# Cross-attention with its row sums computed among the values, reciprocals turned by transfers, and outputs normalized and projected four heads at a time

## The chip, the core and the metric

The kernel runs on one core of a Trainium2 chip. A core has five engines that run side by side: TensorE for matmuls (PE in the profile; its weight loads are PEld), VectorE (DVE), ScalarE (ACT), GpSimd (POOL) and SyncE (SP), which here only issues transfers. They meet at semaphores. Matmuls write to PSUM, eight banks of 128 partitions by 512 floats; all else lives in SBUF. The metric is the device time of one execution in microseconds (us), lower being better.

## What is computed

The reference is two layers on 1024 tokens of width 128, each an attention over a context of 6404 rows (width 96) and a mixture of experts. The change lies in the second attention and what follows it at once:

```python
q = (x @ Wq).reshape(B, S, HEADS, DIM_HEAD).transpose(0, 2, 1, 3)      # 8 heads of 64
k = (context @ Wk).reshape(B, L, HEADS, DIM_HEAD).transpose(0, 2, 1, 3)
v = (context @ Wv).reshape(B, L, HEADS, DIM_HEAD).transpose(0, 2, 1, 3)
attn = jnp.einsum('bhsd,bhld->bhsl', q, k) * scale
attn = jax.nn.softmax(attn, axis=-1)
out = jnp.einsum('bhsl,bhld->bhsd', attn, v)
out = out.transpose(0, 2, 1, 3).reshape(B, S, INNER)
return out @ Wo + bo
```

The result is added to x; a layer norm and the last mixture of experts follow.

## The kernel before, in words

**Stages.** A start (loads, layer norm, first projections), the maxima of the first attention's scores and the value projection for all heads (values go to a DRAM scratch), the first attention, the first experts, a stretch in which the maxima of head 0 are found, then the second attention from 347 to 1326 us of the span, then the second experts. Each engine has its own program, written out by hand in the order in which it runs; there is no scheduler. An instruction that waits holds up all that is behind it on its engine.

**The second attention.** The 6404 context rows are 51 tiles of 126. The loop runs over 8 heads (h) and, in each, over 13 blocks (b) of four tiles (the last has three). In a block PE does, in this order: the scores of tiles against all 1024 queries, two halves of 512 (`scores1`, L1406 and L1407, the second matmul adding the low parts and the shift by the row's maximum); two steps of the maxima of the next head (`max_scores`, L1372); the product with the values for each tile (`attend1`, L1419, one matmul for each half of the queries, into the two halves of the partitions of bank 7); after the first tile of these the key projection for a later head (`k_proj_parts`, L1359); and two more maxima steps. ACT takes exp of each score bank (`exps`, L718) and rounds the projected keys (L683). DVE reduces the maxima steps from PSUM (`maxima`, L959), makes the low parts of the keys (L949) and adds the exps of one tile in four to the second half of the row sums (`add_rows`, L1011, L1016); POOL adds the rest (L527, L531) and folds DVE's part in (L536). From here on, "head 2, block 4" is h = 2, b = 4; a block is counted from its first L1406 to that of the next. A block with nothing special in it is called plain.

**What is done once a head**, in the middle of blocks after the third tile's scores: in block 1 the row sums of the head before (`sum_rows`, eight matmuls that have 128 columns of the summed exps as weights and one column of ones as data, L1432) and their reciprocals on DVE (L980); in blocks 2 and 3 the output projection of the head before (`project_out`, L1444, two halves of four matmuls each) and on DVE the scaled addition to x (`add_output`, L990); in blocks 5 and 6 a query projection for two heads on (L1351, L671, L943); in block 12 the shifts of the next head: DVE's row maxima are turned by one matmul (`row_shift`, L1377, into bank 5), and DVE spreads them over eight rows of q_low (`shift`, L970). Bank 5 is also one of the two banks of the maxima step behind, so that step waits for DVE. ACT copies the head's output from bank 7 to `acc_raw` (L692). `c_reduced`, `c_exped`, `c_shift`, `c_x`, `c_out` are the semaphores by which PE waits for maxima, exps, shifts and additions.

**SP** issues all transfers in one order: at each head's start the values of a later head (1.6 MB), then wq and wk.

**Where PE waits for DVE in each block.** The bank of the fourth score (tile 1, second half) and of the fifth are those of the first maxima step, and after the third tile's scores PE waits for both steps; so a DVE that is late with the maxima holds PE up.

## Time and profile before

| | us |
|---|---|
| three runs | 1439.64, 1443.58, 1443.79 |
| median | 1443.58 |
| the profiled execution, its own time | 1445.09 |
| its span, first to last instruction | 1443.3 |
| TensorE, mean granted clock | 0.975 |

The span is 1.8 us shorter than that execution's own time. Busy shares say that PE is nearly always occupied, but a busy PE is not one at its peak, as its matmuls overlap. What a once-a-head piece costs is read best from the length of its block against a plain one.

### The profile page before, as it was taken

What the parts mean: (1) busy time and instruction counts of PE and PEld (TensorE: products, weight loads), DVE (VectorE), ACT (ScalarE), POOL (GpSimd) and SP (SyncE); (2) the same over time, 40 slices, a digit from 0 to 9 for tenths busy, and PEclk for the clock granted to TensorE, in tenths of its full rate; (3) what the DMA queues carried; (4) which work ended last, traced back from release to release, by engine and by line L of the source; (5) the groups of instructions that cost most, each with busy time, mean ns of one, the idle gap of its engine ahead of it and who ended that gap; (6) DMA issues with size and microseconds to landing.
All of it is one profiled execution on the core that took longest, in us unless ns stands there. A gap on an engine that the chain in (4) does not pass through costs nothing.

```text
span 1443.3 us, 20175 instructions
## 1 busy us (share of the span) xinstructions
PE 1382.9 (96%) x6309; PEld 797.2 (55%) x6309; DVE 1095.1 (76%) x1484; ACT 796.0 (55%) x1580; POOL 943.4 (65%) x543
## 2 busy tenths in 40 slices
PE   5989998887999999999999999999999999999898
PEld 3867776533455555555555555555555555555665
DVE  8976666597887778788777978787887887676655
ACT  3458887322565555556555555555555565554432
POOL 5001112342889889888988988898888899887110
PEclk8999999966999999999999999999999999999999
DMA  6640000400000200200020020002002000000011
GB/s 172 206 134 17 17 17 8 92 4 0 1 1 1 50 1 1 49 1 1 1 50 1 1 49 1 1 1 50 0 1 47 0 1 0 1 1 13 19 41 39
DMA packets 77373, 39.46 MB, mean 27 GB/s; under 512 B 62047, under 2 KB 70000, under 8 KB 77002
## 3 DMA queue, kind: packets, MB, share of 16 engines
q1 hardware_dynamic: 77290, 38.36, 10.6%
q8 instruction: 52, 0.85, 0.2%
q14 instruction: 31, 0.25, 0.1%
HBM read 24.66 MB, written 13.68 MB: 27 GB/s over the span
## 4 chain that ended last, share of the span: by engine, by line
PE 87%; DVE 7%; DMA 3%; ACT 2%; issue 1%; POOL 0%; SPq 0%; ACTq 0%; DVEq 0%; POOLq 0%
PE ps L1419 25%; PE ps L1406 15%; PE ps L1407 13%; PE ps L1372 9%; DVE chunk_max L959 3%; DMA v_scratch<-v_stage 3%; PE ps L1359 3%; PE ps L1577 2%; PE ps L1239 2%; PE ps L1240 2%; PE ps L1241 2%; PE ps L1228 2%; PE ps L1230 2%; PE ps L1229 2%; PE ps L1563 1%
## 5 line engine op out<-in xcount | busy, mean ns | idle before, releaser
L531 POOL TENSOR_TENSOR psums<-psums,probs 126x1024 f32<-126x1024 f32 (+1 forms) x392 | 821.6, 2096 | 122.9 <-ACT probs L718 75.4
L718 ACT ACTIVATE probs<-ps 126x512 f32<-126x512 f32 (+1 forms) x816 | 416.9, 617 | 290.5 <-PE ps L1407 287.0
L959 DVE TENSOR_REDUCE chunk_max<-ps 128x2 f32<-128x1008 f32 (+1 forms) x416 | 472.5, 1181 | 75.7 <-PE ps L1372 74.3
L1419 PE MATMUL ps<-probs,v_mem 126*64 126x512 f32 (+1 forms) x1632 | 389.6, 598 | 0.0
L1406 PE MATMUL ps<-q_heads,ring 128*126 128x512 f32 (+1 forms) x816 | 343.1, 420 | 1.2
L1407 PE MATMUL ps<-q_low,ring 128*126 128x512 f32 (+1 forms) x816 | 322.6, 395 | 0.0
L1011 DVE TENSOR_TENSOR xn<-xn,probs 126x512 f32<-126x512 f32 x126 | 231.8, 1840 | 29.9 <-ACT probs L718 25.6
L683 ACT CAST ring<-ps 64x252 fp32r<-64x252 f32 (+1 forms) x356 | 128.4, 361 | 136.2 <-PE ps L1359 133.0
L1419 PEld LDWEIGHTS ps<-probs,v_mem 126*64 126x64 f32 (+1 forms) x1632 | 111.5, 136 | 165.5 <-issue 121.2
L1406 PEld LDWEIGHTS ps<-q_heads,ring 128*126 128x126 f32 (+1 forms) x816 | 152.1, 186 | 88.4 <-issue 43.9
L1372 PE MATMUL ps<-ring,q_heads 64*128 64x504 f32 (+1 forms) x416 | 169.3, 475 | 19.1 <-DVE chunk_max L959 10.6
L1407 PEld LDWEIGHTS ps<-q_low,ring 128*126 128x126 f32 (+1 forms) x816 | 153.0, 188 | 32.8 <-issue 2.9
L1372 PE MATMUL ps<-ring,q_low 64*128 64x504 f32 (+1 forms) x416 | 169.3, 475 | 0.0
L1372 PEld LDWEIGHTS ps<-ring,q_heads 64*128 64x128 f32 x416 | 70.1, 194 | 160.1 <-issue 71.6
L485 POOL TENSOR_TENSOR wv_lo<-vslot,wv_hi 126x97 fp32r<-126x97 f32 x51 | 20.4, 399 | 185.9 <-DVE wv_hi L858 185.9
L863 DVE TENSOR_TENSOR q_shift<-probs,q_all 126x512 fp32r<-126x512 f32 x102 | 70.5, 693 | 58.8 <-ACT q_all L612 58.6
L949 DVE TENSOR_TENSOR ring<-ps,ring 64x252 fp32r<-64x252 f32 (+1 forms) x178 | 73.7, 414 | 34.4 <-ACT ring L683 32.2
L1372 PEld LDWEIGHTS ps<-ring,q_low 64*128 64x128 f32 x416 | 70.1, 194 | 0.0
L612 ACT ACTIVATE q_all<-ps 126x512 fp32r<-126x512 f32 x102 | 60.9, 599 | 11.1 <-PE ps L1241 1.4
L605 ACT ACTIVATE probs<-ps 126x512 f32<-126x512 f32 x102 | 60.7, 601 | 9.7 <-PE ps L1230 2.9
L829 DVE TENSOR_REDUCE chunk_max<-ps 128x1 f32<-128x378 f32 x136 | 63.1, 542 | 2.1 <-PE ps L1194 2.0
L540 POOL TENSOR_TENSOR parts<-pair_w,parts 128x256 fp32r<-128x256 f32 x17 | 11.9, 703 | 73.8 <-ACT parts L744 73.8
(212 smaller groups left out, 1422.7 us busy)
## 6 DMA issues: line engine op xcount, KB each, us to landing
v_scratch<-v_stage SPq DMA_DIRECT2D x51, 252.0 KB
v_mem<-v_scratch SPq DMA_DIRECT2D x8, 1606.5 KB
ctx_mem<-in_ctx_t SPq DMA_DIRECT2D x3, 803.2 KB, 8.8
vslot<-in_ctx_rows SPq DMA_DIRECT2D x51, 47.2 KB
pair_w<-in_f_pairs SPq DMA_DIRECT2D x17, 128.0 KB, 2.1
pair_w<-in_f_pairs SPq DMA_DIRECT2D x17, 65.0 KB, 1.8
x_tok<-in_x SPq DMA_DIRECT2D x1, 512.0 KB, 4.2
wo<-in_c_wo SPq DMA_DIRECT2D x1, 512.0 KB
```

The source lines that it names most:

```text
L531: pool.tensor_tensor(sums[0:r, 0:width], sums[0:r, 0:width], probs[0:r, n % PROBS, 0:width], ALU.add).then_inc(c_sum, 1)
L683: ins = act.copy(ring[half * HD:(half + 1) * HD, g % RING, tiles, 0, :], ps[part * HD:(part + 1) * HD, bank, 0:(tiles.stop - tiles.start) ...
L718: act.activation(probs[0:r, n % PROBS, cols(half)], ps[0:r, score_bank(t, half), :], ACT.Exp, scale=float(HD) ** -0.5).then_inc(c_exped, 1)
L829: dve.tensor_reduce(chunk_max0[:, i, g:g + 1], ps[:, i % 4, 0:CK], AX, ALU.max).then_inc(max_reduced, 1)
L863: dve.tensor_tensor(p_lo[:, cols(half)], probs0[:, j, cols(half)], f32(p_hi[:, cols(half)]), ALU.subtract).then_inc((a_plo0, a_padd)[half] ...
L949: ins = dve.tensor_tensor(ring[HD:P, g % RING, tiles, 1, :], ps[rows, bank, 0:(tiles.stop - tiles.start) * KT] .rearrange("p (n k) -> p n ...
L959: dve.tensor_reduce(chunk_max[:, h % 2, i:i + 2, c], ps[:, banks[0]:banks[1] + 1, 0:group_tiles(c) * KT], AX, ALU.max).then_inc(c_reduced, 1)
L1011: dve.tensor_tensor(sums[0:r, :], sums[0:r, :], new[0:r, :], ALU.add).then_inc(c_sumd, 1)
L1372: pe.matmul(ps[:, banks[half], 0:group_tiles(c) * KT], q[rows, h % 3, tile_cols(i + half)], ring[rows, g % RING, 0:group_tiles(c), 0, :], ...
L1406: pe.matmul(s, ring[:, g % RING, j, 0, 0:r], q_heads[:, h % 3, cols(half)], start=True, stop=False)
L1407: pe.matmul(s, ring[:, g % RING, j, 1, 0:r], q_low[:, h % 3, cols(half)], start=False, stop=True).then_inc(c_scored, 1)
L1419: ins = pe.matmul(ps[half * HD:(half + 1) * HD, B_ACC, :], v_tiles[0:r, h % 2, t, :], probs[0:r, n % PROBS, cols(half)], start=(t == 0), s ...
```

## The change

1. `sum_rows` becomes, for heads 0 to 6, two matmuls with ones (126 by 64) as weights and 512 columns of summed exps as data, so that each of 64 partitions holds all sums of a half; they stand behind the key projection among the value products of block 1 and write to bank 1 (for head 6 bank 5). ACT copies the bank to SBUF (`sums_out`).
2. SP turns the sums by way of DRAM (`turn_sums`): a write of 2 rows of 512, a read back as 128 by 8 (32 bytes a partition), DVE's reciprocal of 128 by 8 in block 2 behind the row additions, a write of these, and two reads that spread them over 64 partitions each.
3. DVE multiplies the head's output (128 by 512, in SBUF) by them in block 4 (`normalize`). The outputs of four heads stay in `acc`.
4. The output projections of heads 0 to 3 are done at once, in head 4, block 7, added up in PSUM over the heads; DVE adds two banks to x. Those of heads 4 to 7 follow the last block, head 7 on its own and scaled as before.
5. `row_shift` goes to bank 1, one of the banks of the scores, ahead of the third tile's scores; the maxima step behind no longer waits for the shift.
6. The first loads of the experts' weights (pair_w, four transfers) move from the start to the end of the second attention, and some small buffers change place; the memset of q_low and the flipped identity report by another semaphore.

TensorE, block 12 of a head (L1377 and in the changed program L1434 is the turning of the row maxima, L1406/L1466 the scores of the third tile, L1372/L1429 the maxima steps), before and then changed:

```order
L1406 MATMUL ps<-q_heads,ring 104x512
L1407 MATMUL ps<-q_low,ring 104x512
L1377 MATMUL ps<-neg_ident,row_max 8x128
L1372 MATMUL ps<-ring,q_heads 128x504
L1372 MATMUL ps<-ring,q_low 128x504
L1372 MATMUL ps<-ring,q_heads 128x504
L1372 MATMUL ps<-ring,q_low 128x504
L1419 MATMUL ps<-probs,v_mem 64x512 x2
```
```order
L1434 MATMUL ps<-neg_ident,row_max 8x128
L1466 MATMUL ps<-q_heads,ring 104x512
L1467 MATMUL ps<-q_low,ring 104x512
L1466 MATMUL ps<-q_heads,ring 104x512
L1467 MATMUL ps<-q_low,ring 104x512
L1429 MATMUL ps<-ring,q_heads 128x504
L1429 MATMUL ps<-ring,q_low 128x504
L1429 MATMUL ps<-ring,q_heads 128x504
```
The turning has moved ahead of the third tile's four score matmuls.

TensorE, block 1 of a head (L1432: row sums before; L1489: row sums changed; L1419/L1479: value products; L1359/L1416: key projection), before and then changed:

```order
L1432 MATMUL ps<-ones,psums 128x1 x8
L1406 MATMUL ps<-q_heads,ring 126x512
L1407 MATMUL ps<-q_low,ring 126x512
L1406 MATMUL ps<-q_heads,ring 126x512
L1407 MATMUL ps<-q_low,ring 126x512
L1372 MATMUL ps<-ring,q_heads 128x504
L1372 MATMUL ps<-ring,q_low 128x504
L1372 MATMUL ps<-ring,q_heads 128x504
L1372 MATMUL ps<-ring,q_low 128x504
L1419 MATMUL ps<-probs,v_mem 64x512 x2
L1359 MATMUL ps<-ctx_mem,wk 64x252 x2
```
```order
L1466 MATMUL ps<-q_heads,ring 126x512
L1467 MATMUL ps<-q_low,ring 126x512
L1429 MATMUL ps<-ring,q_heads 128x504
L1429 MATMUL ps<-ring,q_low 128x504
L1429 MATMUL ps<-ring,q_heads 128x504
L1429 MATMUL ps<-ring,q_low 128x504
L1479 MATMUL ps<-probs,v_mem 64x512 x2
L1416 MATMUL ps<-ctx_mem,wk 64x252 x2
L1489 MATMUL ps<-psums,ones 64x512 x2
L1479 MATMUL ps<-probs,v_mem 64x512 x6
```
The row sums have left the scores and stand among the value products, as two matmuls in the place of eight.

VectorE, blocks 2 to 4 (L990: scaled addition to x; L1011/L1065: row additions; L1018: reciprocals; L1026: normalize; L959/L999: maxima; L949/L989: low parts of keys), before and then changed:

```order
L959 TENSOR_REDUCE chunk_max<-ps 128x2 x2
L990 SCALAR_TENSOR_TENSOR x_tok<-ps,rden,x_tok 128x128 x4
L1011 TENSOR_TENSOR xn<-xn,probs 126x512
L959 TENSOR_REDUCE chunk_max<-ps 128x2 x2
L949 TENSOR_TENSOR ring<-ps,ring 64x2x126 x2
L959 TENSOR_REDUCE chunk_max<-ps 128x2 x2
L990 SCALAR_TENSOR_TENSOR x_tok<-ps,rden,x_tok 128x128 x4
L1011 TENSOR_TENSOR xn<-xn,probs 126x512
L959 TENSOR_REDUCE chunk_max<-ps 128x2 x2
L949 TENSOR_TENSOR ring<-ps,ring 64x2x126 x2
L959 TENSOR_REDUCE chunk_max<-ps 128x2 x2
L1011 TENSOR_TENSOR xn<-xn,probs 126x512
```
```order
L1065 TENSOR_TENSOR xn<-xn,probs 126x512
L1018 RECIPROCAL rden<-sum_cols 128x8
L999 TENSOR_REDUCE chunk_max<-ps 128x2 x2
L989 TENSOR_TENSOR ring<-ps,ring 64x2x126 x2
L999 TENSOR_REDUCE chunk_max<-ps 128x2 x2
L1065 TENSOR_TENSOR xn<-xn,probs 126x512
L999 TENSOR_REDUCE chunk_max<-ps 128x2 x2
L989 TENSOR_TENSOR ring<-ps,ring 64x2x126 x2
L999 TENSOR_REDUCE chunk_max<-ps 128x2 x2
L1065 TENSOR_TENSOR xn<-xn,probs 126x512
L1026 TENSOR_TENSOR acc<-acc,xn 128x512
L999 TENSOR_REDUCE chunk_max<-ps 128x2 x2
```
The two scaled additions of blocks 2 and 3 are gone; in their place come a reciprocal behind block 2's row addition and a multiplication behind block 4's.

The diff, cut to its core:

```diff
+B_SHIFT = 1
+B_SUMS = (1, 1, 1, 1, 1, 1, 5, 0)
+BATCH, BATCH_AT = 4, 7
...
@@ sync @@
-            for s in range(2):
-                sp.dma_start(pair_w[:, s, 0:2 * P], f1_pairs[s][:, 0:2 * P]).then_inc(g_w13[s], 16)
-                sp.dma_start(pair_w[:, s, 2 * P:PAIR_W], f1_pairs[s][:, 2 * P:PAIR_W]).then_inc(g_w[s], 16)
...
+            def turn_sums(h):
+                sp.wait_ge(c_spread, h + 1)
+                sp.dma_start(sums_dram[h % 2], spread_sums[0:P:HD, h % 2, :]).then_inc(c_turn, 16)
+                sp.wait_ge(c_turn, 80 * h + 16)
+                sp.dma_start(sum_cols[:, :], sums_dram[h % 2].rearrange("a (p j) -> (a p) j", j=TT)).then_inc(c_turn, 16)
+                sp.wait_ge(c_rden, 2 * h + 1)
+                sp.dma_start(rden_dram[h % 2].rearrange("a (p j) -> (a p) j", j=TT), rden[:, :]).then_inc(c_turn, 16)
+                sp.wait_ge(c_turn, 80 * h + 48)
+                for half in range(2):
+                    sp.dma_start(spread_sums[half * HD:(half + 1) * HD, h % 2, :],
+                                 rden_dram[h % 2, half:half + 1, :].to_broadcast([HD, HALF])).then_inc(c_turn, 16)
+            next_weights(2)
+            for h in range(2, HEADS + 1):
+                if h < HEADS:
+                    sp.wait_ge(c_attended, TILES * (h - 1))
+                    sp.dma_start(v_tiles[:, h % 2], v_dram_v[h]).then_inc(c_vload[h % 2], 16)
+                if h + 1 < HEADS:
+                    next_weights(h + 1)
+                turn_sums(h - 2)
@@ scalar @@
-                if h:
-                    act.wait_ge(c_out, 2 * h)
-                act.copy(acc_raw[:, :], ps[:, B_ACC, :]).then_inc(c_acc, 1)
+                if h >= BATCH:
+                    act.wait_ge(c_out, 1)
+                act.copy(acc[:, h % BATCH, :], ps[:, B_ACC, :]).then_inc(c_acc, 1)
+            def sums_out(h):
+                act.wait_ge(c_sums, h + 1)
+                act.copy(spread_sums[:, h % 2, :], ps[:, B_SUMS[h], :]).then_inc(c_spread, 1)
...
+                    if b == 1 and h:
+                        sums_out(h - 1)
@@ vector @@
             def reciprocals(h):
...
+                if h < HEADS - 1:
+                    dve.wait_ge(c_turn, 80 * h + 32)
+                    dve.reciprocal(rden[:, :], sum_cols[:, :]).then_inc(c_rden, 1)
...
+            def normalize(h):
+                dve.wait_ge(c_turn, 80 * h + 80)
+                dve.wait_ge(c_acc, h + 1)
+                dve.tensor_tensor(acc[:, h % BATCH, :], acc[:, h % BATCH, :], spread_sums[:, h % 2, :],
+                                  ALU.mult).then_inc(c_rden, 1)
+            def add_outputs(n):
+                dve.wait_ge(c_out, 2 * n + 1)
...
+                for half in range(2):
+                    tiles = slice(half * (TT // 2), (half + 1) * (TT // 2))
+                    ins = dve.tensor_tensor(x_tok[:, tiles, :],
+                                            ps[:, PAIRS[1][half], :].rearrange("p (t d) -> p t d", d=D),
+                                            x_tok[:, tiles, :], ALU.add)
...
-                    if b == 1 and h:
-                        reciprocals(h - 1)
-                    if b in (2, 3) and h:
-                        add_output(h - 1, b - 2, PAIRS[1])
+                    if (h, b) == (BATCH, BATCH_AT):
+                        add_outputs(0)
...
+                    if b == 2 and h:
+                        reciprocals(h - 1)
+                    if b == 4 and h:
+                        normalize(h - 1)
...
             reciprocals(HEADS - 1)
-            for part in range(2):
-                add_output(HEADS - 1, part, PAIRS[part])
+            add_last_output()
+            dve.wait_ge(c_x, 2)
+            add_outputs(1)
@@ tensor @@
+                if h and t == 2 * GT and k == B_SUMS[h - 1]:
+                    pe.wait_ge(c_spread, h)
...
+                if h < HEADS - 1:
+                    for half in range(2):
+                        ins = pe.matmul(ps[half * HD:(half + 1) * HD, B_SUMS[h], :], ones[0:KT, 0:HD], psums[:, h % 2, cols(half)],
+                                        start=True, stop=True)
...
+            def project_out(h, banks, first, last):
+                for u in range(TT // 2):
+                    for half in range(2):
+                        rows = slice(half * HD, (half + 1) * HD)
+                        ins = pe.matmul(ps[:, banks[half], tile_cols(u)], acc[rows, h % BATCH, tile_cols(u)], wo1[rows, h, :],
+                                        start=(first and u == 0), stop=last, skip_group_check=True)
+                return ins
...
+                        if b == GROUPS_H - 1 and t % GT == 1 and h + 1 < HEADS:
+                            pe.wait_ge(c_exped, 2 * (TILES * h + b * GT) + B_SHIFT + 1)
+                            row_shift(h + 1, B_SHIFT)
...
-                            if b == 1 and h:
-                                sum_rows(h - 1)
-                            if b in (2, 3) and h:
-                                if b == 3:
-                                    pe.wait_ge(c_x, 2 * h - 1)
-                                project_out(h - 1, b - 2, PAIRS[1])
+                            if (h, b) == (BATCH, BATCH_AT):
+                                pe.wait_ge(c_rden, 2 * BATCH)
+                                for done in range(BATCH):
+                                    ins = project_out(done, PAIRS[1], done == 0, done == BATCH - 1)
+                                ins.then_inc(c_out, 1)
...
-                            if b == GROUPS_H - 1 and h + 1 < HEADS:
-                                row_shift(h + 1)
...
-                        elif b == GROUPS_H - 1 and h + 1 < HEADS:
-                            pe.wait_ge(c_shift, 2 * h + 4)
...
-                        if t % GT == 0 and g is not None:
+                        if t % GT == 0 and (g is not None or (b == 1 and h)):
                             pe.wait_ge(c_exped, 2 * (TILES * h + block_tiles(b)[-1] + 1))
-                            k_proj_parts(g, B_KEYS)
-            pe.wait_ge(c_x, 2 * HEADS - 2)
-            for part in range(2):
-                project_out(HEADS - 1, part, PAIRS[part])
+                            if g is not None:
+                                k_proj_parts(g, B_KEYS)
+                            if b == 1 and h:
+                                sum_rows(h - 1)
+            project_out(BATCH, PAIRS[1], True, False)
+            pe.wait_ge(c_acc, HEADS)
+            project_out(HEADS - 1, PAIRS[0], True, True).then_inc(c_out, 1)
             sum_rows(HEADS - 1)
+            project_out(BATCH + 1, PAIRS[1], False, False)
+            project_out(BATCH + 2, PAIRS[1], False, True).then_inc(c_out, 1)
```

## Rows read from the trace of the kernel before

**Rows 1.** The page's first part: busy us, share, instructions.
```profile
PE 1382.9 (96%) x6309; PEld 797.2 (55%) x6309; DVE 1095.1 (76%) x1484; ACT 796.0 (55%) x1580; POOL 943.4 (65%) x543
```
**Rows 2.** The page's fourth part, the chain that ended last, by engine.
```profile
PE 87%; DVE 7%; DMA 3%; ACT 2%; issue 1%; POOL 0%; SPq 0%; ACTq 0%; DVEq 0%; POOLq 0%
```
**Rows 3.** Stretches: start:end length, busy by engine, clock, DMA; head 2.
```profile
610.98:622.01 11.03, 11.03 (x63) 6.62 (x61) 7.81 (x9) 5.59 (x12) 8.41 (x4) 1.00 0.01 1
622.01:632.18 10.17, 10.17 (x55) 5.42 (x53) 8.61 (x11) 5.59 (x12) 7.73 (x4) 1.00 0.00 1
632.18:642.65 10.47, 10.33 (x54) 5.26 (x53) 9.04 (x12) 5.70 (x12) 8.96 (x5) 1.00 0.01 2
642.65:651.94 9.29, 9.29 (x46) 4.76 (x45) 8.07 (x9) 5.49 (x12) 7.62 (x4) 1.00 0.00 0
...
601.65:728.05 126.40, 125.28 (x605) 66.06 (x603) 100.41 (x105) 73.35 (x159) 109.93 (x52) 1.00 0.07 15
```
**Rows 4.** The same view: head 7, its blocks 1, 2 and 4.
```profile
1234.90:1244.16 9.26, 9.26 (x50) 5.75 (x49) 7.55 (x6) 4.13 (x8) 8.54 (x6) 1.00 0.00 0
1244.16:1252.51 8.35, 8.35 (x42) 4.42 (x41) 5.36 (x8) 4.13 (x8) 7.33 (x6) 1.00 0.01 3
...
1260.84:1268.32 7.48, 7.48 (x34) 3.96 (x32) 5.02 (x4) 4.03 (x8) 5.57 (x5) 1.00 0.00 0
```
**Rows 5.** TensorE in time order, head 2: start, us, line, [idle before <- releaser].
```profile
607.64 2.74 PE L1419 MATMUL ps<-probs,v_mem 126*64 126x512 f32 x12
...
613.86 1.84 PE L1432 MATMUL ps<-ones,psums 126*128 126x1 f32 x16
...
624.99 0.71 PE L1444 MATMUL ps<-wo,acc_raw 64*128 64x128 f32 x8
```
**Rows 6.** TensorE in time order, block 12 of head 2.
```profile
722.04 0.39 PE L1377 MATMUL ps<-neg_ident,row_max 128*8 128x128 f32 x2
722.50 0.50 PE L1372 MATMUL ps<-ring,q_heads 64*128 64x504 f32 x1
...
723.79 0.50 PE L1372 MATMUL ps<-ring,q_heads 64*128 64x504 f32 x1 [0.79 <-DVE q_low L970]
```
**Rows 7.** VectorE in time order, head 2: blocks 4 and 5, then 12.
```profile
645.13 2.49 DVE L1011 TENSOR_TENSOR xn<-xn,probs 126x512 f32<-126x512 f32 x1
...
650.35 0.85 DVE L949 TENSOR_TENSOR ring<-ps,ring 64x252 fp32r<-64x252 f32 x2 [0.49 <-ACT ring L683]
651.85 2.32 DVE L959 TENSOR_REDUCE chunk_max<-ps 128x2 f32<-128x1008 f32 x2 [0.65 <-PE ps L1372]
656.50 0.69 DVE L943 TENSOR_TENSOR q_heads<-ps,q_heads 64x512 fp32r<-64x512 f32 x1 [2.33 <-ACT q_heads L671]
...
722.46 1.28 DVE L970 TENSOR_TENSOR q_low<-ps,diag 8x512 fp32r<-8x512 f32 x2 [1.19 <-PE ps L1377]
```
**Rows 8.** Durations by line, in ns: least, median, most.
```profile
L1011 DVE TENSOR_TENSOR xn<-xn,probs x126: 668/1738/2748, 374.1 to 1325.2; 126x512 f32<-126x512 f32 x125, 104x512 f32<-104x512 f32 x1
...
L531 POOL TENSOR_TENSOR psums<-psums,probs x392: 1271/2367/2725, 354.1 to 1326.3; 126x1024 f32<-126x1024 f32 x132, 126x512 f32<-126x512 f32 x60, 104x1024 f32<-104x1024 f32 x4
...
L929 DVE TENSOR_TENSOR x_tok<-ps,x_tok x2: 681/686/692, 270.7 to 271.3; 128x512 f32<-128x512 f32 x2
```
**Rows 9.** ScalarE in time order, the key casts of head 2, block 4.
```profile
648.82 1.50 ACT L683 CAST ring<-ps 64x252 fp32r<-64x252 f32 x4 [1.29 <-PE ps L1359]
```
**Rows 10.** The transfers: size and median us from issue to landing.
```profile
wq<-in_c_wq SPq DMA_DIRECT2D x8, 64.0 KB, 9.8
out_t<-ctx_mem SPq DMA_DIRECT2D x2, 256.0 KB, 2.0
...
gw<-in_f_gw SPq DMA_DIRECT2D x1, 16.0 KB, 1.6
```
**Rows 11.** All engines in time order, behind the second attention.
```profile
1327.27 1.16 PE L1444 MATMUL ps<-wo,acc_raw 64*128 64x128 f32 x16 [0.78 <-ACT acc_raw L692]
...
1330.66 2.16 DVE L990 SCALAR_TENSOR_TENSOR x_tok<-ps,rden,x_tok 128x128 f32<-128x128 f32 x8
```

114 lines of the change are left out of this document (53 added, 61 removed).

## Prediction, on record before the result was known

> **What bounds the kernel now.** I read the page's busy shares first: PE is busy for 96% of the span, DVE for 76%, POOL for 65% [rows 1]. A busy PE is no proof that it is the bound, so next the chain that ended last: 87% of it is PE [rows 2]. What counts is then how long each block takes, so I cut head 2 into stretches that begin at a block's first score matmul. A plain block (block 4) takes 9.29 us; in it PE is busy throughout, DVE for 8.07 [rows 3]. Block 1, with the row sums of the head before, takes 11.03; blocks 2 and 3, with the two halves of the output projection, 10.17 and 10.47. So these pieces lie in the open, and each costs what its block is longer: 1.74, 0.88 and 1.18 us. The other heads from 1 to 6 show the same blocks. In head 7, where there are no maxima left to find, block 4 takes 7.48, block 1 9.26 and block 2 8.35 [rows 4]: 1.78 and 0.87 more. Block 12 has a hole of its own: after the turning of the row maxima the second maxima step starts 1.29 us behind the first, 0.79 of it idle time that DVE's shift ends [rows 6].
>
> The sum is made against the profiled execution's 1445.1 us, which is 1.5 above the median of the runs, 1443.6; 1.8 of it lie outside the span.
>
> **Row sums.** Sixteen PE instructions (eight matmuls of two passes) in 1.84 us [rows 5] become four of the same shape as the value products of one tile, of which three tiles (twelve instructions) take 2.74 [rows 5]: 0.9 us. Gain in heads 1 to 6: 6 x (1.74 - 0.9) = 5.0; in head 7: 0.9. ACT's copy of the bank goes where ACT has just cast the keys and waits for the next block's scores; ACT is busy for 5.49 of a plain block's 9.29 [rows 3], so it costs nothing.
>
> **Output projection in blocks 2 and 3.** Both go: 6 x (0.88 + 1.18) = 12.4, and in head 7 twice 0.87, 1.7. Their work comes back in two places. The batch in head 4, block 7 has 32 matmuls, 64 instructions; at the rate of the tail (16 in 1.16 us [rows 11]) that is 4.6, at that of a block (8 in 0.71 [rows 5]) 5.7; I take 5.1. Behind it DVE adds two banks, each an addition of 128x512 from PSUM at 0.69 [rows 8], and PE has a tile's scores and one maxima step to do meanwhile, about the same length: 0.4 more. Together 5.5, once.
>
> **Reciprocals by way of DRAM.** DVE now waits in block 2 for a write and a read of 4 KB, and the maxima behind it wait with it. In a plain block DVE is through with the row addition at 645.13 + 2.49 = 647.62, 4.97 us into it [rows 7]. Block 1 will be 10.2 long, so DVE comes to the reciprocals 15.2 us after block 1 began. ACT ends its key casts at 648.82 + 1.50, 7.67 us into a block [rows 9], and copying a bank costs under 0.78 (PE's idle time ahead of the projection of the tail is such a copy [rows 11]): the sums are in SBUF at 8.4. That leaves 6.8 us for two transfers. A write to DRAM of 256 KB lands after 2.0 us, a small read after 1.6 [rows 10], so about 4 with the issues. The wait should be nothing. From both sides: zero, and if each took as long as wq's 9.8 [rows 10], about 12 us a head. I take zero, since wq's is long only because it is issued right behind the 1.6 MB of values; those go at the start of block 0, some 17 us ahead of the sums. The spreading back has two blocks of time. The Trainium skill (DMA: Bandwidth & Descriptors, Anatomy of one DMA) gives some 2.0 us as the fixed cost of a transfer and calls DRAM the slowest target; by it the round trip would be near 4, and with the landings above the trace agrees. The same page's Specifications want pieces of 512 bytes or more and speak of read-modify-write below; the writing back of the reciprocals is in pieces of 32 bytes, and no row here shows what such a write costs.
>
> **Normalizing in block 4.** DVE gains a multiplication of 128x512 with both inputs in SBUF. Its nearest rows are the row additions of 126x512: at least 0.67 us, 1.74 in the middle, 2.75 at most [rows 8]. The spread comes from POOL, which adds 126x1024 at 2.37 at a time nearly without a pause: where a DVE addition falls on a POOL one, it ends after it. The new one directly follows a row addition, so it meets the next POOL addition: 2.4 us is my value; the bounds are 0.67 and 2.37 + 0.67 = 3.04. In a plain block DVE idles for 0.49 and 0.65 [rows 7], 1.14 together. So DVE is 2.4 - 1.14 = 1.3 us late with the maxima of block 5, of which PE, which has a little time there, loses 1.1. A hint that the lateness counts: block 3 has the same PE work as block 2, DVE is busy for 0.43 us more, and the block is 0.30 longer [rows 3]. In block 5 DVE idles 2.33 ahead of the query's low part [rows 7] and catches up. Cost: 6 x 1.1 = 6.6, between 0 and 6 x (3.04 - 1.14) = 6 x 1.9 = 11.4. In head 7 DVE is busy for 5.02 of 7.48 [rows 4], which hides it.
>
> **Shifts by way of a bank of scores.** Head 2's 0.79 us goes [rows 6]: the turning starts some 1 us earlier, DVE, idle 1.19 ahead of the shift [rows 7], starts it as much earlier, and the maxima step no longer shares its bank. The exp of the first tile, for which PE now waits, should be just through. What is late next is DVE's row addition, which then meets POOL at another point; nothing to 0.79 is left. I take all of it, in six heads (0 to 5): 4.7.
>
> **The tail.** The projection of head 4 goes ahead of the wait for ACT's copy: 1.16 for the 0.78 idle [rows 11], 0.4 more. Those of heads 5 and 6 lie beside DVE's reciprocals and additions (2.16 [rows 11]), but then two additions of 0.69 [rows 8] follow in the open: 1.4. Together 1.8. The weights loaded late are used well behind the layer norm. Fewer loads at the start may give up to 1 us; I take none.
>
> **Sum.** Gains 5.0 + 0.9 + 12.4 + 1.7 + 4.7 = 24.7. Costs 5.5 + 6.6 + 1.8 = 13.9. Net 10.8: 1445.1 to 1434.3, and 1443.6 to 1432.8 in terms of the median.
>
> **Rivals.**
> The round trip through DRAM is too long (the slower one). DVE stands in block 2 of heads 1 to 7 with all maxima behind it. It starts to cost when both transfers take more than 6.8 + 1.1 = 7.9 us, and eats up the whole gain at 10.8 / 7 = 1.5 more, 9.4 us, 4.7 for each. At 5 each it would be 7 x 2.1 = 14.7, so 1432.8 + 14.7 = 1447.5. For it: wq's 9.8 us, and no 32-byte write in the trace. Against it: every small transfer with nothing ahead lands in about 2. Chance 0.07.
>
> VectorE becomes the bound. The normalizing costs its upper end, 11.4 for 6.6, and the row addition of block 12, which now starts 1 us earlier, falls on a POOL addition and gives the 4.7 back: 1432.8 + 4.8 + 4.7 = 1442.3. For it: in a head of 126.40 us DVE is busy 100.41 and POOL 109.93 [rows 3], and the head shrinks while both have as much to do. Against it: 11 us of slack are left on POOL even in a head of 121. Chance 0.08.
>
> The normalizing always waits for a whole POOL addition, 2.37 + 0.67 = 3.04, and block 12 keeps its gain: 6 x (1.9 - 1.1) = 4.8 more, 1437.6. For it: the addition before it holds POOL back, so POOL is next when it ends. Against it: 2.75 is the most that any row addition took [rows 8]. Chance 0.12. The Trainium skill (SBUF — State Buffer, Who interferes with whom) has this as a rule: a two-input VectorE operation from SBUF and a GpSimd operation that reads SBUF exclude each other for a whole instruction. The spread of the row additions agrees with it; how the two take turns when DVE has two in a row beside 1024-wide ones, no row shows.
>
> The normalizing falls into a gap of POOL or into DVE's idle time: 0.67 is under 1.14, it costs nothing, 1432.8 - 6.6 = 1426.2. For it: the least of 0.67 does occur. Against it: the row addition before it ends just when POOL goes on. Chance 0.14.
>
> **How the numbers follow.** The forecast has 0.55; the rest, 0.04, is for what I don't see. A change is told from none at about 0.3%, 4.3 us. Faster: forecast, gap and the whole wait (0.81) and half of the unseen, 0.83. Same: the bound case and the other half, 0.10. Slower: 0.07. The range from 1426 to 1440 takes in the gap case and the whole wait and stops short of the bound case.
>
> **What would show it.** Block 1 of head 2 near 10.2 us, blocks 2 and 3 near 9.3, block 5 longer by about 1.1 than now, block 12 shorter by 0.8; the batch block 5.5 us longer; DVE with no wait for a transfer ahead of the reciprocals; the normalizing at 2.4 us. It is wrong if DVE waits for the read of the sums, if a block other than 5 grows, or if the tail costs more than 3 us.

## The result, and the profile after

| | before | changed |
|---|---|---|
| median, us (lowest to highest, 4 runs each) | 1443.37 (1439.64 to 1443.79) | 1429.40 (1427.00 to 1431.47) |
| ratio | | 0.9905, 95% interval 0.9891 to 0.9919 |
| the profiled execution, its own time | 1445.09 | 1430.34 |
| its span | 1443.3 | 1428.5 |
| mean granted clock | 0.975 | 0.975 |

The changed kernel is faster: by 14.0 us in the medians (11.7 to 15.7 by the interval) and by 14.8 between the two traces. Forecast were 10.8, just below that interval, and 1432.8 us; the time lies inside the range of 1426 to 1440. The median before is that of four runs, one more than the prediction had.

First the busy shares of the changed kernel, beside [rows 1].

```profile
PE 1371.8 (96%) x6225; PEld 784.4 (55%) x6225; DVE 1103.8 (77%) x1439; ACT 798.7 (56%) x1587; POOL 944.2 (66%) x543
```

PE is busy for 11.1 us less. DVE is busy for 8.7 more with 45 instructions fewer: 56 scaled additions of 128x128 went, 7 multiplications and 4 additions of 128x512 came. That is the first hint at where part of the gain stays. Next the stretches of the changed kernel, cut at the same instructions as [rows 3] and [rows 4]: head 1 blocks 1 to 5 and the whole head; head 2 block 4 and the whole head; head 4 block 7; head 7 blocks 1 and 2.

```profile
480.38:490.53 10.15, 10.15 (x51) 5.14 (x49) 7.84 (x8) 6.07 (x13) 7.74 (x5) 1.00 0.01 1
490.53:499.78 9.25, 9.25 (x46) 4.83 (x44) 8.17 (x9) 5.48 (x12) 7.66 (x4) 1.00 0.02 3
499.78:509.01 9.23, 9.23 (x46) 4.85 (x44) 8.09 (x8) 5.49 (x12) 8.66 (x5) 1.00 0.12 28
509.01:519.47 10.46, 9.59 (x46) 4.91 (x44) 10.38 (x8) 5.49 (x12) 9.74 (x6) 1.00 0.00 0
519.47:530.26 10.79, 10.61 (x48) 5.21 (x46) 8.43 (x10) 6.19 (x13) 9.27 (x5) 1.00 0.01 2
471.05:595.23 124.18, 122.78 (x576) 63.60 (x574) 102.44 (x98) 73.73 (x160) 110.17 (x52) 1.00 0.08 17
...
633.15:642.38 9.23, 9.23 (x47) 4.84 (x45) 8.90 (x9) 5.49 (x12) 8.66 (x5) 1.00 0.01 2
595.23:717.82 122.59, 122.17 (x577) 63.61 (x575) 95.60 (x98) 73.64 (x160) 110.60 (x52) 1.00 0.08 18
...
911.52:925.06 13.54, 13.54 (x110) 8.40 (x108) 8.62 (x11) 6.59 (x13) 9.30 (x5) 1.00 0.01 1
...
1220.14:1228.65 8.51, 8.51 (x39) 4.16 (x37) 6.85 (x5) 4.61 (x9) 7.79 (x7) 1.00 0.00 0
1228.65:1236.14 7.49, 7.49 (x34) 3.96 (x33) 5.62 (x6) 4.03 (x8) 6.92 (x5) 1.00 0.02 1
```

Blocks 1, 2 and 3 have come down to 10.15, 9.25 and 9.23, the last two to the length of a plain block. Block 4, plain before at 9.29 [rows 3], is now 10.46, with PE busy for only 9.59 of it and DVE for 10.38. Head 2 is the exception: its block 4 is 9.23 and the head 1.6 us shorter than head 1. The block with the batch is 13.54, where heads 1, 3 and 5 have 9.47 or 9.48. The lengths of all heads, cut in this way:

| us | head 0 | 1 | 2 | 3 | 4 | 5 | 6 | 7 (blocks 0 to 11) |
|---|---|---|---|---|---|---|---|---|
| before | 128.10 | 126.51 | 126.40 | 126.40 | 126.74 | 126.41 | 119.82 | 93.31 |
| changed | 126.74 | 124.18 | 122.59 | 124.09 | 128.18 | 124.20 | 118.37 | 90.86 |
| normalizing on GpSimd (below) | 126.87 | 122.63 | 123.25 | 122.62 | 126.71 | 122.63 | 116.80 | 90.86 |

Why block 4 grew is seen in VectorE's time order in the changed kernel, block 4 of head 1 and then of head 2:

```profile
511.28 2.71 DVE L1065 TENSOR_TENSOR xn<-xn,probs 126x512 f32<-126x512 f32 x1
513.91 2.84 DVE L1026 TENSOR_TENSOR acc<-acc,xn 128x512 f32<-128x512 f32 x1
516.68 2.31 DVE L999 TENSOR_REDUCE chunk_max<-ps 128x2 f32<-128x1008 f32 x2
...
635.40 0.72 DVE L1065 TENSOR_TENSOR xn<-xn,probs 126x512 f32<-126x512 f32 x1
636.04 2.87 DVE L1026 TENSOR_TENSOR acc<-acc,xn 128x512 f32<-128x512 f32 x1
```

and in TensorE's, at the end of block 4 of head 1:

```profile
517.93 0.50 PE L1429 MATMUL ps<-ring,q_heads 64*128 64x504 f32 x1 [0.26 <-DVE chunk_max L999]
...
519.04 0.50 PE L1429 MATMUL ps<-ring,q_heads 64*128 64x504 f32 x1 [0.61 <-DVE chunk_max L999]
```

GpSimd's additions beside them, two in head 1 and one in head 2:

```profile
511.03 2.41 POOL L565 TENSOR_TENSOR psums<-psums,probs 126x1024 f32<-126x1024 f32 x1
513.59 2.62 POOL L565 TENSOR_TENSOR psums<-psums,probs 126x1024 f32<-126x1024 f32 x1
...
634.28 1.29 POOL L565 TENSOR_TENSOR psums<-psums,probs 126x512 f32<-126x512 f32 x1
```

In head 1 the row addition and the normalizing (L1026) take 2.71 and 2.84 us in a row, and the maxima start so late that PE waits for them twice, 0.87 together. Each of the two starts while a GpSimd addition is running and ends about 0.55 behind it: 513.99 behind 513.44, 516.75 behind 516.21. In head 2 the row addition, in the same code, starts when GpSimd's addition has 0.17 left and takes 0.72, again ending 0.55 behind it. DVE is 2 us earlier with everything behind it, and PE waits for nothing, though the normalizing itself takes 2.87. What shifts GpSimd against DVE in head 2 the runs don't say.

The round trip through DRAM, in the queue's rows of the changed kernel for head 2, then ScalarE's and VectorE's:

```profile
612.81 0.51 SPq L429 DMA_DIRECT2D sums_scratch<-xn  x1
614.40 0.34 SPq L431 DMA_DIRECT2D sum_cols<-sums_scratch  x1
617.75 0.32 SPq L433 DMA_DIRECT2D rden_scratch<-rden  x1
619.16 1.12 SPq L436 DMA_DIRECT2D xn<-rden_scratch  x2
...
612.20 0.59 ACT L730 COPY xn<-ps 128x512 f32<-128x512 f32 x1
...
617.53 0.20 DVE L1018 RECIPROCAL rden<-sum_cols 128x8 f32<-128x8 f32 x1
```

SP issues each transfer when the one before has landed, so the distance of two rows bounds a landing: at most 1.6 us for the write of the sums, at most 1.4 for that of the reciprocals in pieces of 32 bytes. That holds for heads 2 to 7; in head 1 3.2 pass behind the write of the reciprocals, and no run shows why. The reciprocals' row has no idle time in any head.

### The profile page after: what moved, and what is told of

The parts are those of the page before. It is cut to its first block, busy times and chain, and to the rows that moved or that the text cites. A ratio compares the mean times of both kernels' runs of the same rounds, so it can differ in the third digit from the quotient of the medians.

```text
span 1428.5 us, 19977 instructions
## 1 busy us (share of the span) xinstructions
PE 1371.8 (96%) x6225; PEld 784.4 (55%) x6225; DVE 1103.8 (77%) x1439; ACT 798.7 (56%) x1587; POOL 944.2 (66%) x543
## 4 chain that ended last, share of the span: by engine, by line
PE 84%; DVE 9%; DMA 4%; ACT 2%; issue 1%; SPq 0%; POOL 0%; DVEq 0%; ACTq 0%; POOLq 0%
PE ps L1479 24%; PE ps L1466 14%; PE ps L1467 12%; PE ps L1429 9%; DVE chunk_max L999 4%; DMA v_scratch<-v_stage 3%; PE ps L1416 3%; PE ps L1642 2%; PE ps L1287 2%; PE ps L1285 2%; PE ps L1286 2%; PE ps L1296 2%; PE ps L1297 2%; PE ps L1298 2%; PE ps L1629 1%; PE ps L1628 1%
## 5 line engine op out<-in xcount | busy, mean ns | idle before, releaser
L999 DVE TENSOR_REDUCE chunk_max<-ps 128x2 f32<-128x1008 f32 (+1 forms) x416 | 472.3, 1180 | 87.6 <-PE ps L1429 86.3
L1479 PE MATMUL ps<-probs,v_mem 126*64 126x512 f32 (+1 forms) x1632 | 389.8, 598 | 0.0
L1466 PE MATMUL ps<-q_heads,ring 128*126 128x512 f32 (+1 forms) x816 | 340.7, 418 | 0.9
L1065 DVE TENSOR_TENSOR xn<-xn,probs 126x512 f32<-126x512 f32 x126 | 236.1, 1873 | 24.2 <-ACT probs L756 19.4
L1479 PEld LDWEIGHTS ps<-probs,v_mem 126*64 126x64 f32 (+1 forms) x1632 | 111.6, 136 | 169.3 <-issue 118.5
L1466 PEld LDWEIGHTS ps<-q_heads,ring 128*126 128x126 f32 (+1 forms) x816 | 151.9, 186 | 86.8 <-issue 45.3
L1429 PE MATMUL ps<-ring,q_heads 64*128 64x504 f32 (+1 forms) x416 | 168.8, 475 | 19.0 <-DVE chunk_max L999 13.9
L1429 PE MATMUL ps<-ring,q_low 64*128 64x504 f32 (+1 forms) x416 | 169.0, 475 | 0.0
L1429 PEld LDWEIGHTS ps<-ring,q_heads 64*128 64x128 f32 x416 | 69.3, 195 | 160.5 <-issue 74.4
L989 DVE TENSOR_TENSOR ring<-ps,ring 64x252 fp32r<-64x252 f32 (+1 forms) x178 | 73.7, 414 | 38.3 <-ACT ring L717 35.9
L1429 PEld LDWEIGHTS ps<-ring,q_low 64*128 64x128 f32 x416 | 69.3, 195 | 0.0
```

What stands on the lines that cost most here:

```text
L989: ins = dve.tensor_tensor(ring[HD:P, g % RING, tiles, 1, :], ps[rows, bank, 0:(tiles.stop - tiles.start) * KT] .rearrange("p (n k) -> p n ...
L999: dve.tensor_reduce(chunk_max[:, h % 2, i:i + 2, c], ps[:, banks[0]:banks[1] + 1, 0:group_tiles(c) * KT], AX, ALU.max).then_inc(c_reduced, 1)
L1065: dve.tensor_tensor(sums[0:r, :], sums[0:r, :], new[0:r, :], ALU.add).then_inc(c_sumd, 1)
L1429: pe.matmul(ps[:, banks[half], 0:group_tiles(c) * KT], q[rows, h % 3, tile_cols(i + half)], ring[rows, g % RING, 0:group_tiles(c), 0, :], ...
L1466: pe.matmul(s, ring[:, g % RING, j, 0, 0:r], q_heads[:, h % 3, cols(half)], start=True, stop=False)
L1479: ins = pe.matmul(ps[half * HD:(half + 1) * HD, B_ACC, :], v_tiles[0:r, h % 2, t, :], probs[0:r, n % PROBS, cols(half)], start=(t == 0), s ...
```

## The experiments

Each kernel was traced and, where a ratio stands, timed beside the kernel before.

**Normalizing 8 of 512 columns.** Does the multiplication cost its own work, or the wait for the addition that GpSimd is at? This kernel scales 8 of the head's 512 columns and leaves the others unscaled.

```diff
-                dve.tensor_tensor(acc[:, h % BATCH, :], acc[:, h % BATCH, :], spread_sums[:, h % 2, :],
+                dve.tensor_tensor(acc[:, h % BATCH, 0:8], acc[:, h % BATCH, 0:8], spread_sums[:, h % 2, 0:8],
                                   ALU.mult).then_inc(c_rden, 1)
```

> The changed kernel, but the normalizing multiplies 8 of the 512 columns (the others are left unscaled). It stands at the same place of VectorE, directly behind a row addition. Theory A (what costs is the wait for GpSimd's running addition, 2.37 us, not the multiplication itself): it still takes some 2.2 to 2.4 us, block 4 of heads 1, 3, 4, 5 and 6 stays near 10.0 to 10.4 us, and the time is within 2.5 us of the changed kernel's 1429.4. Theory B (the length of the multiplication counts): it takes about 0.1 us, block 4 falls to 9.3, and the time is about 7 us lower, 1422.

Measured: 1428.69 us, ratio 0.991 [0.9881, 0.9940]. VectorE in block 4 of head 1 of this kernel:

```profile
510.74 2.71 DVE L1065 TENSOR_TENSOR xn<-xn,probs 126x512 f32<-126x512 f32 x1
513.38 2.32 DVE L1026 TENSOR_TENSOR acc<-acc,xn 128x8 f32<-128x8 f32 x1
```

and GpSimd beside the multiplication:

```profile
513.05 2.62 POOL L565 TENSOR_TENSOR psums<-psums,probs 126x1024 f32<-126x1024 f32 x1
```

With a sixty-fourth of the elements it still takes 2.32 us, and ends at 515.70, 0.03 behind GpSimd's addition: 2.3 of the 2.84 are waiting, 0.5 work. Block 4 is 9.92 to 9.97 in the heads where it was 10.45 to 10.48, the 0.5 that it has less to do, and still 0.7 above a plain one. Making the operation smaller hardly helps.

**Normalizing left out.** A reduction of 8 numbers, which reads one tensor, takes its place; outputs of heads 0 to 6 stay unscaled.

```diff
-                dve.tensor_tensor(acc[:, h % BATCH, :], acc[:, h % BATCH, :], spread_sums[:, h % 2, :],
-                                  ALU.mult).then_inc(c_rden, 1)
+                dve.tensor_reduce(acc[:, h % BATCH, 0:1], acc[:, h % BATCH, 0:8], AX, ALU.max).then_inc(c_rden, 1)
```

> The changed kernel with the normalizing left out: in its place a reduction of 8 numbers, with one input. Both theories: the whole price of the normalizing is gone, block 4 near 9.3 us in every head, blocks 5 and 7 0.3 shorter, and the time is five heads times 1.5 = 7.5 us lower, about 1422. If it is lowered by less than 4 us, the stall of block 4 has another cause.

Measured: 1421.25 us, ratio 0.9848 [0.9826, 0.9870], 8.2 below the changed kernel. VectorE in block 4 of head 1 of this kernel, and that block's stretch:

```profile
511.18 2.73 DVE L1064 TENSOR_TENSOR xn<-xn,probs 126x512 f32<-126x512 f32 x1
513.83 0.15 DVE L1026 TENSOR_REDUCE acc<-acc 128x1 f32<-128x8 f32 x1
...
508.92:518.17 9.25, 9.25 (x47) 4.83 (x45) 8.19 (x9) 5.49 (x12) 8.68 (x5) 1.00 0.00 0
```

At the same place behind the same row addition the reduction goes through in 0.15, where the 8-column multiplication took 2.32. Block 4 is plain in every head. So this is the whole price of the normalizing: heads 1 to 7 sum to 825.3 us here and to 832.5 in the changed kernel, 7.2. It is made up of 1.5 to 1.6 in each of heads 1, 3, 4, 5 and 6, and of 0.6 the other way in head 2, which is 123.15 here and 122.59 with the normalizing (its blocks 5 and 6 are longer without it, 10.86 and 10.78). The rest of the 8.2 lies outside these heads.

**Normalizing ahead of the queries' low part.** DVE idles 2.33 us in block 5 waiting for the query cast [rows 7]; this version puts the multiplication there (for head 5, in block 12 of head 6).

```diff
+                    if h and b == (GROUPS_H - 1 if h == HEADS - 2 else 5):
+                        normalize(h - 1)
                     if b in (5, 6) and h + 2 < HEADS:
                         q_lo(h + 2, b - 5, B_AUX)
...
-                    if b == 4 and h:
-                        normalize(h - 1)
```

> The changed kernel with the normalizing moved to block 5, ahead of the query's low part, where VectorE idles for 2.2 to 2.3 us (in head 6 to block 12, ahead of the shift, where it idles for 4.0). Theory: it runs in that hole and costs at most 0.5 us a head in place of 1.5; block 4 falls to 9.3, block 5 grows by 0 to 0.5; the time is 5 to 7 us lower, about 1423.5. Rival: the query's low part is late by as much as before and TensorE waits for it in block 5 instead; the time stays at 1429.

Measured: 1424.72 us, ratio 0.9877 [0.9847, 0.9906], 4.7 below the changed kernel. VectorE in block 5 of head 1:

```profile
522.12 2.70 DVE L1026 TENSOR_TENSOR acc<-acc,xn 128x512 f32<-128x512 f32 x1
524.85 0.69 DVE L983 TENSOR_TENSOR q_heads<-ps,q_heads 64x512 fp32r<-64x512 f32 x1
```

It lasts nearly as long as before (2.70 for 2.84), but now in time that was idle, and the low part starts right behind it; block 4 is 9.25 and block 5 10.85 in head 1. Against the kernel without the normalizing 0.4 us remain of the 1.5 in each of heads 1, 3, 4 and 5 and nothing in head 6. The duration hardly changed, only what stood behind it. The 4.7 lie just under the 5 to 7 that were expected, but heads 1 to 7 sum to 826.2, 6.2 less than in the changed kernel.

**Normalizing on GpSimd.** If the price is the wait for GpSimd, GpSimd itself can multiply between two of its additions.

```diff
+                    if h and t == 4 * GT:
+                        pool.wait_ge(c_turn, 80 * h)
+                        pool.wait_ge(c_acc, h)
+                        done = acc[:, (h - 1) % BATCH, :]
+                        pool.tensor_tensor(done, done, spread_sums[:, (h - 1) % 2, :], ALU.mult).then_inc(c_rden, 1)
...
+                    dve.wait_ge(c_rden, 2 * (h - 1))
...
-                    if b == 4 and h:
-                        normalize(h - 1)
```

> The changed kernel with the normalizing given to GpSimd, ahead of its addition for tile 16 of the next head. Theory (what costs is VectorE standing behind GpSimd's running addition; GpSimd itself may lag by some 10 us before anyone waits for it): the multiplication takes about 1.3 us there, blocks 4 are 9.3 us in all heads, and the time is that of the kernel with the normalizing left out, 1421 to 1422, with everything computed. Rival (GpSimd, busy for 823 of some 980 us, has no room, and the exps wait for its sums): blocks 5 to 8 grow by more than 0.3 us each and the time stays at 1427 or above.

Measured: 1421.34 us (1418.64 to 1422.66), ratio 0.9855 [0.9835, 0.9876]: the fastest complete version, 8.1 below the changed kernel and 20.9 below the kernel before. GpSimd in block 4 of head 1 of this version, VectorE beside it, and the block's stretch:

```profile
511.12 1.31 POOL L557 TENSOR_TENSOR acc<-acc,xn 128x512 f32<-128x512 f32 x1
512.38 9.29 POOL L570 TENSOR_TENSOR psums<-psums,probs 126x1024 f32<-126x1024 f32 x4
...
511.54 1.44 DVE L1064 TENSOR_TENSOR xn<-xn,probs 126x512 f32<-126x512 f32 x1
513.76 2.32 DVE L1004 TENSOR_REDUCE chunk_max<-ps 128x2 f32<-128x1008 f32 x2 [0.78 <-PE ps L1427]
...
509.28:518.53 9.25, 9.25 (x47) 4.83 (x45) 6.92 (x8) 5.49 (x12) 8.82 (x6) 1.00 0.00 0
```

The multiplication takes GpSimd 1.31 us, and DVE's row addition beside it 1.44 rather than 2.71. DVE waits for PE again ahead of the maxima, not PE for DVE, and block 4 is plain in all heads. The row addition again ends 0.55 behind GpSimd's operation (512.98 behind 512.43). The time equals that of the kernel without the normalizing, though in these heads GpSimd has the most to do after PE (111.3 of head 1's 122.6 us): its slack, 11 us a head, takes it up.

Not all of the 8.1 is the edit's. Heads 1 to 7 sum to 825.5 us, 7.0 less than in the changed kernel; in the traces the part from the layer norm on is 2.8 shorter too (108.7 for 111.5), though its code is the same. Its first 27.14 us here:

```profile
1310.36:1337.50 27.14, 23.44 (x128) 18.68 (x127) 19.47 (x100) 12.59 (x18) 5.00 (x5) 1.00 0.07 18
```

The granted clock is 1.00 here, and 0.94 in the same stretch of the changed kernel, which is shown further down. So by the heads alone this place is worth 7.0 and the one ahead of the low part 6.2, 0.7 less; between the medians the two differ by 3.4.

**The shifts alone.** The kernel before, with nothing but the turning of the row maxima moved to bank 1, ahead of the third tile's scores.

```diff
+                        if b == GROUPS_H - 1 and t % GT == 1 and h + 1 < HEADS:
+                            pe.wait_ge(c_exped, 2 * (TILES * h + b * GT) + 2)
+                            row_shift(h + 1, 1)
...
-                            if b == GROUPS_H - 1 and h + 1 < HEADS:
-                                row_shift(h + 1)
...
-                        elif b == GROUPS_H - 1 and h + 1 < HEADS:
-                            pe.wait_ge(c_shift, 2 * h + 4)
```

> The kernel before with only the turning of the row maxima moved to bank 1 and ahead of the third tile's scores. My theory: block 12 of heads 0 to 5 goes from 9.0 to 8.3 us as in the changed kernel, nothing else changes, the time is 4 us lower, 1438.5. Rival (the gain of block 12 came from the additions to x that are gone, or VectorE's row addition there gives it back): block 12 stays above 8.8 and the time within 1.5 us of before.

Measured: 1439.31 us over 10 runs, ratio 0.9976 [0.9966, 0.9985]. TensorE in block 12 of head 2 of this kernel, to be set beside [rows 6]:

```profile
720.41 0.47 PE L1372 MATMUL ps<-ring,q_heads 64*128 64x504 f32 x1 [0.28 <-issue]
720.72 0.39 PE L1372 MATMUL ps<-ring,q_heads 64*128 64x504 f32 x1
```

The second maxima step starts 0.31 behind the first, not 1.29; 0.28 of idle time, for which the profile names no releaser, stand ahead of the first. Block 12 is 8.29 to 8.33 in heads 0 to 5, as in the changed kernel, and 6.20 in head 6 (6.04 before). The rest of this kernel is as before, so this part of the gain is its own, 3 to 4 us (2.9 between the medians, 3.9 by the blocks).

**The late weights alone.** The changed kernel's first score of the second attention comes at 344.31 us, 2.7 earlier than before (347.04), and that was not in the sum. One candidate is the four weight loads that moved away from the start. This is the kernel before with those alone moved.

```diff
-            for s in range(2):
-                sp.dma_start(pair_w[:, s, 0:2 * P], f1_pairs[s][:, 0:2 * P]).then_inc(g_w13[s], 16)
-                sp.dma_start(pair_w[:, s, 2 * P:PAIR_W], f1_pairs[s][:, 2 * P:PAIR_W]).then_inc(g_w[s], 16)
...
                 sp.dma_start(dst, src).then_inc(in_f1, 16)
+            for s in range(2):
+                sp.dma_start(pair_w[:, s, 0:2 * P], f1_pairs[s][:, 0:2 * P]).then_inc(g_w13[s], 16)
+                sp.dma_start(pair_w[:, s, 2 * P:PAIR_W], f1_pairs[s][:, 2 * P:PAIR_W]).then_inc(g_w[s], 16)
```

> The kernel before with only the first four loads of the experts' weights moved from the start to the end of the second attention. Theory A (these loads stood in the way of the first stores of values): the second attention's scores begin 2.7 us earlier than at 347.0, as in the changed kernel, and the time is 2 to 3 us lower, 1441. Theory B (the 2.7 us were one late store in the trace of before, at 73 us): no hole of 2.7 us in ScalarE's copies and the start at 344 to 345, but the same time as before within 1 us in the median, since its other runs have no such hole either.

Measured: 1443.70 us over 10 runs, ratio 1.0006 [0.9991, 1.0020]: the loads give nothing that can be told. Its first score came at 344.78 all the same, which points at the trace of before, not at the loads.

**The kernel before, traced again.** Its code is unchanged.

> The kernel before as it is, traced a second time, for the start. In the first trace of it ScalarE stands idle for 2.73 us at 76.04 waiting for a store, the first stage ends its row maxima at 94.60 and the first score of attention 2 begins at 347.04; seven later traces, of other kernels, have 91.35 to 93.85 and 344.10 to 346.19. Theory A (a store that came late in that one execution): this trace has no idle of over 2.1 us there, the maxima end at 91.5 to 94.0, and the first score begins at 344 to 346; the blocks behind it are as in the first trace (126.4 us a head). Theory B (the start of the kernel before is slower by its code): the hole of 2.7 us is there again and the first score begins at 346.8 to 347.3.

Measured: 1442.30 us in one run. TensorE's first score and ScalarE's longest wait for a store of values, first in this second trace, then (one row each) in the first trace of the kernel before:

```profile
344.69 0.79 PE L1406 MATMUL ps<-q_heads,ring 128*126 128x512 f32 x1
...
90.57 0.58 ACT L596 COPY v_stage<-ps 126x512 f32<-126x512 f32 x1 [1.07 <-DMA v_scratch<-v_stage]
```
```profile
347.04 0.79 PE L1406 MATMUL ps<-q_heads,ring 128*126 128x512 f32 x1
...
76.04 1.97 ACT L596 COPY v_stage<-ps 126x512 f32<-126x512 f32 x3 [2.73 <-DMA v_scratch<-v_stage]
```

The same code now starts at 344.69 without the hole of 2.73, and its blocks have the old lengths (126.46 for head 1). So 2.4 of the 2.7 us at the start are a matter of the one execution and belong to neither kernel; over all the traces the first score comes between 344.10 and 347.04. The late store explains 1.0 of it (the stage it is in ends at 93.63 rather than 94.60); the other 1.4 came between there and the second attention, and the runs don't say where.

**One and two more round trips.** The slower rival was a round trip too long for its place. These kernels send the sums once more, or twice more, through DRAM ahead of the last read; the waits' constants are raised to fit. There is one run of each.

```diff
+                for more in range(1):   # range(2) in the second kernel
+                    sp.dma_start(sum_cols[:, :], sums_dram[h % 2].rearrange("a (p j) -> (a p) j", j=TT)).then_inc(c_turn, 16)
+                    sp.wait_ge(c_turn, 112 * h + 32 * more + 32)
+                    sp.dma_start(more_dram[:, :], spread_sums[0:P:HD, h % 2, :]).then_inc(c_turn, 16)
+                    sp.wait_ge(c_turn, 112 * h + 32 * more + 48)
```

> The changed kernel with one more read and one more write of 4 KB between the write of the sums and their read. In the changed kernel the sums should have landed some 11.4 us after block 1 began, and VectorE comes for them at 15.0; one more round is 3.2 us. Theory (there is room): no wait ahead of the reciprocals, or under 1 us, block 2 at 9.3 us, the time as before the edit. Rival (the room is less than thought, since the trace shows no time of landing): VectorE waits for 1 us or more and block 2 grows.

> The same with two more rounds, 6.4 us. Theory: the sums land at 17.8, VectorE waits for some 2.8 us, 1.1 of which its idle time in a block hides; block 2 or 3 grows by 1.5 to 2 us in heads 1 to 6, and the time by about 10 us to 1439. Rival (nothing in these blocks waits for VectorE): block 2 and 3 stay at 9.3 us.

Measured with one more: 1431.18 us, heads of the same length as in the changed kernel to 0.04 us. Its one wait, in head 2:

```profile
620.08 0.20 DVE L1024 RECIPROCAL rden<-sum_cols 128x8 f32<-128x8 f32 x1 [1.71 <-DMA sum_cols<-sums_scratch]
```

There DVE comes 2 us earlier than in the other heads, behind a row addition of 0.7, so the wait costs nothing, though it is longer than the 1 us that was expected at most.

Measured with two more: 1445.73 us. The queue and VectorE in head 4 of that kernel:

```profile
869.24 0.50 SPq L430 DMA_DIRECT2D sums_scratch<-xn  x1
870.82 0.32 SPq L433 DMA_DIRECT2D sum_cols<-sums_scratch  x1
...
877.22 0.31 SPq L437 DMA_DIRECT2D sum_cols<-sums_scratch  x1
...
873.36 2.70 DVE L1071 TENSOR_TENSOR xn<-xn,probs 126x512 f32<-126x512 f32 x1
878.75 0.20 DVE L1024 RECIPROCAL rden<-sum_cols 128x8 f32<-128x8 f32 x1 [2.69 <-DMA sum_cols<-sums_scratch]
```

Each leg takes 1.6 us from issue to the next issue, and the last 1.5 to 1.7 to the reciprocals in heads 2 to 5, 2.4 and 2.5 in heads 1 and 6. DVE is free at 873.36 + 2.70 = 876.1, which is 6.8 us after the first issue, just the room that the prediction gave. By these legs the changed kernel's two need 3.1 to 4.1 of it (an estimate, since DVE comes later than they land there); one more round trip needs 3.2 more and is at most 0.5 beyond the room, within DVE's 1.1 of idle time; two more need 9.5 to 10.5 and cost 15.4 us over heads 1 to 6, more than the change gains.

By the prediction's edge of 7.9 us, 9.5 should cost 1.6 a head, and heads 3, 4 and 5 lost 1.5 to 1.7. Heads 1, 2 and 6 lost more: 3.6, 3.3 and 3.7. In head 2 DVE comes 2 us earlier, which leaves less room; in heads 1 and 6 the longer last leg explains 0.9 of the 2 us that they lost above the others, and the rest stays open. Head 7, which the rival counted too, lost nothing. So the time was nearly 7 us above the 1439 that was expected. The slower rival is a real mechanism, its edge where it was put for three heads, its cost too low for the other three. The changed kernel stays 3.8 us or more short of that edge.

## Why the prediction was right

Between the medians the gain is 3.2 us more than the sum, by terms that partly cancel; from the first score of the second attention to the layer norm it is 13.1 for the 10.8. Measured are block lengths against the first trace of the kernel before.

- **What bounds the kernel.** Right: what was taken out of PE's order came back at the blocks' own price, and what was added to an engine with slack cost nothing until DVE came late with the maxima.
- **Row sums.** 0.93 us in each of heads 1 to 6 (0.84 forecast) and 0.75 in head 7 (0.9): 6.4 for 5.9. ScalarE's copy of the bank, 0.59, cost nothing.
- **Projections out of blocks 2 and 3.** 12.9 for 12.4, and 1.7 for 1.7 in head 7. Block 3 gave 1.2 and block 2 0.9. The difference fits DVE's lateness going with it, as the hint in [rows 3] had it; no run tests that.
- **The batch.** 13.54 - 9.48 = 4.1 for 5.5. TensorE's row for it in the changed kernel, and VectorE's additions behind:

```profile
914.72 3.84 PE L1503 MATMUL ps<-wo,acc 64*128 64x128 f32 x64
...
918.61 1.29 DVE L1035 TENSOR_TENSOR x_tok<-ps,x_tok 128x512 f32<-128x512 f32 x2 [4.49 <-PE ps L1503]
```

The 64 instructions took 3.84, less than either rate that the working had (4.6 and 5.7), and the two additions lay beside PE's scores, with all but 0.2 hidden.
- **Reciprocals by way of DRAM.** Zero, as taken. The writing of 32-byte pieces, which no row of before could bound, landed within 1.4 us in six heads of seven. The Trainium skill (DMA: Bandwidth & Descriptors, Specifications) speaks of read-modify-write below 512 bytes: at 4 KB these runs show no price for it. The 2.0 us that the same page (Anatomy of one DMA) gives as a transfer's fixed cost are for the path by way of GpSimd, which the prediction did not say; here, where SyncE issues them, most legs took 1.6 and the longest 2.5, apart from head 1's 3.2.
- **Normalizing.** 7.2 for 6.6, nearly right by two misses, so by luck. The operation took 2.84 and not 2.4, and where it stalled PE it cost about 1.5 a head and not 1.1: 1.15 in block 4 and 0.3 in blocks 5 to 7 together. The prediction put the whole stall in block 5 and named a block other than 5 growing as a sign that it is wrong. That sign came: the maxima step for which PE waits, right behind the normalizing, still belongs to block 4. Against that, head 2 paid nothing. The value of 2.4 left out the operation's own work behind the wait; 2.84 lies nearer to the 3.04 of the whole-wait rival, and the 8-column kernel splits it into 2.3 of waiting and 0.5 of work. The rival's mechanism held in all of heads 1 to 6 (2.84 to 2.87), its 3.04 was too long by 0.2. The gap rival's did not hold: in head 2 it was the row addition that met GpSimd near its end, not the normalizing. The Trainium skill (SBUF — State Buffer, Who interferes with whom) has the exclusion as a rule, and these runs agree: a two-input multiplication of 8 columns waits 2.3 us, a one-input reduction at its place takes 0.15.
- **Shifts.** 0.67 a head and not 0.79: in the kernel with the shifts alone the two maxima steps lie 0.98 closer, and 0.28 idle remain ahead of them; 4.0 for 4.7, less 0.2 that head 6 loses.
- **The tail.** 1.4 for 1.8, from the last block to the layer norm. Its rows in the changed kernel:

```profile
1309.22 2.06 PE L1503 MATMUL ps<-wo,acc 64*128 64x128 f32 x32
...
1315.69 1.29 DVE L1035 TENSOR_TENSOR x_tok<-ps,x_tok 128x512 f32<-128x512 f32 x2
```

The two wide additions stand in the open for 1.3, as the working said. Behind them the kernel takes 1.1 us more than before, which was not in the sum. The first 27.14 us from the layer norm on, before and then changed:

```profile
1332.86:1360.00 27.14, 22.68 (x122) 17.94 (x121) 19.49 (x100) 12.58 (x18) 5.01 (x5) 0.98 0.06 17
```
```profile
1317.01:1344.15 27.14, 23.54 (x123) 18.81 (x122) 18.48 (x98) 12.54 (x18) 5.00 (x5) 0.94 0.07 18
```

The granted clock is 0.98 in the first and 0.94 in the second. In the other traces this part's length goes with the clock in the main and not with the new tail. From the layer norm to the end the kernel before took 110.4 in both of its traces (clock 0.98). Kernels whose code is the changed one's from the last block on took 111.5 to 111.6 at a mean clock of 0.96 (changed, ahead of the low part, one more round trip), 110.3 at 0.97 or 0.98 (8 columns, two more round trips) and 108.7 or 108.8 at 0.99 (on GpSimd, left out). The mean clock isn't the whole of it: the kernel before with the late weights took 109.4 at 0.98. What moved the clock was not tested and stays open.

- **The start.** 2.7 that were not forecast, of which 2.4 are chance: against the second trace of before (span 1440.5) the changed kernel's span is 12.0 shorter, close to the 10.8. Another 0.7 is the first block of head 0, 11.4 for 12.1, of which the second trace of before (11.7) shows half as chance too.

The bound, the gains and the free round trip came as worked out; the place of the stall did not. The terms that were off by more than half a microsecond are the batch (1.4 too dear), the normalizing (0.6 too cheap), the shifts (0.7 too good) and the blocks' gains (1.0 too low).

## What to carry to other kernels

Where two engines exclude each other on SBUF as VectorE and GpSimd do here, an operation's size says little about its cost: put it where the engine would idle anyway (6.2 of 7.2 us came back), or give it to the engine it would wait for, if that one has slack (7.0). A round trip through DRAM is free as long as the consumer gets there later than its legs add up; count the legs at their measured length and compare with when the consumer is free. A difference that sits in front of all the code that changed, or behind it, is to be looked for in other traces of the same code, with their granted clock beside it.
